# Second stage: the low parts of key tiles 3 and 7 are subtracted on GpSimd in place of VectorE

## The reference, cut to what matters

```python
def _L2_attn_ref(seq):
    attn = jnp.einsum('blc,bmc->blm', seq, seq)
    attn = jax.nn.softmax(attn, axis=2)
    return jnp.einsum('blm,bmc->blc', attn, seq)
...
t = t + _L2_attn_ref(_ln_t(t))
```

## Time and profile before

| | |
|---|---|
| median of 3 runs | 3016.01 us (3010.62 to 3026.71) |
| the profiled execution, its own time | 3013.47 us |
| its span, first to last instruction | 3011.3 us |
| VectorE busy over the span | 2327.7 us (77%) |
| PE busy | 2282.4 us (76%) |
| ScalarE busy | 2132.5 us (71%) |
| GpSimd busy | 1742.0 us (58%) |
| granted TensorE clock, mean over the span | 0.923 |
| `low`, line 1166, 256 instructions | 319.4 us, mean 1269 ns |
| the subtraction of the same shape on GpSimd in a later stage, line 1813, 256 instructions | 544.9 us, mean 2142 ns |

### The profile page before, as it was taken

One profiled execution on the slowest core, in us unless ns is written; L12 is line 12 of the kernel. 1 busy time (PEld: TensorE's weight loads), 2 busy tenths in 40 slices (PEclk: granted clock), 3 DMA queues, 4 the chain that ended last, 5 costly groups with the idle time before them and its releaser, 6 DMA issues. The chain is left out here.

```text
span 3011.3 us, 86006 instructions
## 1 busy us (share of the span) xinstructions
PE 2282.4 (76%) x33244; PEld 1642.6 (55%) x33244; DVE 2327.7 (77%) x3714; ACT 2132.5 (71%) x3776; POOL 1742.0 (58%) x1370
## 2 busy tenths in 40 slices
PE   3777777778774888888644585888888888777777
PEld 1555555555552655555433473776777676545444
DVE  3677778777774999999867325888888887688897
ACT  2677777777773999999722112888888887777776
POOL 3577777777764333333266202998999898733331
PEclk9999999999996999999957556999999999899999
DMA  3211111111100000000000200000000000000101
GB/s 72 49 44 42 36 37 39 42 42 31 27 16 4 18 17 14 17 17 15 12 1 1 52 5 2 9 5 5 6 7 5 5 7 7 4 22 21 24 21 25
DMA packets 144669, 62.22 MB, mean 21 GB/s; under 512 B 118676, under 2 KB 127798, under 8 KB 144566
## 3 DMA queue, kind: packets, MB, share of 16 engines
q1 hardware_dynamic: 139565, 58.00, 9.0%
q10 hardware_dynamic: 4393, 2.77, 0.4%
q0 software_dynamic: 608, 0.01, 0.0%
HBM read 14.50 MB, written 8.39 MB: 8 GB/s over the span
## 5 line engine op out<-in xcount | busy, mean ns | idle before, releaser
L1813 POOL TENSOR_TENSOR a_prl<-a_pr,a_prh 128x1024 f16<-128x1024 f32 x256 | 544.9, 2142 | 47.8 <-ACT a_prh L1790 46.1
L1730 DVE TENSOR_REDUCE a_nmax<-a_ps_a 128x1 f16<-128x1024 f32 x256 | 312.2, 1219 | 34.0 <-PE a_ps_a L1852 32.1
L1166 DVE TENSOR_TENSOR a_exl<-a_ex,a_exh 128x1024 f16<-128x1024 f32 x256 | 319.4, 1269 | 8.4 <-ACT a_exh L1219 6.2
L1213 ACT ACTIVATE a_ex<-a_ps_s,a_shift 128x1024 f32<-128x1024 f32 x256 | 281.5, 1101 | 21.1 <-DVE a_exl L1166 12.8
L1790 ACT ACTIVATE a_prh<-a_pr 128x1024 f16<-128x1024 f32 x256 | 270.6, 1057 | 8.1
L1868 PE MATMUL a_ps_s<-a_qx,a_kh 128*128 128x128 f16 x2048 | 259.1, 220 | 2.7 <-issue 2.6
L1786 ACT ACTIVATE a_pr<-a_ps_s 128x1024 f32<-128x1024 f32 x256 | 259.5, 1014 | 0.0
L1870 PE MATMUL a_ps_s<-a_qm,a_kl 128*128 128x128 f16 x2048 | 259.2, 220 | 0.0
L2115 ACT ACTIVATE f_mixed_s<-f_ps_e,f_gates 128x64 f32<-128x64 f32 x1024 | 212.7, 426 | 40.1 <-PE f_ps_e L395 37.2
L113 POOL TENSOR_TENSOR a_w_hl<-a_w_xn,a_w_hl 128x512 f16<-128x512 f32 (+1 forms) x64 | 82.4, 1288 | 273.2 <-ACT a_w_hl L106 273.2
L1274 PEld LDWEIGHTS a_ps_o<-a_w_hl,a_exh 128*128 128x128 f16 x2048 | 181.9, 98 | 91.2 <-DVE a_exl L1166 66.2
(11 more groups left out here) (344 smaller groups left out, 8526.7 us busy)
## 6 DMA issues: line engine op xcount, KB each, us to landing
tokens<-in_x_dram SPq DMA_DIRECT2D x32, 256.0 KB, 2.9
bl_qg<-bl_qk_high SPq DMA_DIRECT2D x128, 64.0 KB, 2.0
bl_km<-bl_qk_high SPq DMA_DIRECT2D x256, 32.0 KB, 2.0
a_xTb<-a_w_xT SPq DMA_DIRECT2D x64, 128.0 KB
out_dram<-tokens SPq DMA_DIRECT2D x32, 256.0 KB, 2.6
bl_qg<-bl_qk_low SPq DMA_DIRECT2D x64, 64.0 KB, 2.0
bl_km<-bl_qk_low SPq DMA_DIRECT2D x128, 32.0 KB, 2.0
a_qm<-a_qx SPq DMA_DIRECT2D x64, 64.0 KB, 2.0
```

Of the source, the lines that this page charges most:

```text
L1166: nc.vector.tensor_tensor(exl[:, at[2]], ex[:, r], exh[:, at[2]], ALU.subtract).then_inc(low, 1)
L1213: nc.scalar.activation(ex[:, r], ps_s[:, m % 2], ACT.Exp, bias=shift[:], accum_out=rs[at[1]][:, m:m + 1]).then_inc(exped, 1)
L1730: nc.vector.tensor_reduce(nmax[:, g:g + 1], ps_a[:], AX.X, ALU.max, negate=True).then_inc(maxed, 1)
L1813: nc.gpsimd.tensor_tensor(prl[:, r], pr[:, r], prh[:, r], ALU.subtract).then_inc(low, 1)
```

## The change

A tuple `POOL_LOW = (3, 7)` names two key tiles whose low part GpSimd now makes, with the same instruction and operands. GpSimd gets a `step` of its own with a lag of one tile: the low part of tile 7 of the image before stands at m=0, ahead of everything else of GpSimd in the image; that of tile 3 stands at m=4, behind lines 90 and 92 and ahead of `norm_apply`. It waits there for the high part. The semaphore `low` becomes two, `low_v` and `low_g`, and the function `low_count` gives for a tile which of the two to wait for and up to which count; ScalarE's ring and TensorE's products wait by it. Nothing else is changed; the last low part of the stage is made in the trailing steps (`lag` 1 for GpSimd's `stream`).

```diff
--- before.py
+++ after.py
@@ -1080,6 +1080,7 @@
 
     nc, sem = net.nc, net.sem
     RING, PARTS, LAG = 4, 8, 4
+    POOL_LOW = (3, 7)
     VECTOR_HIGH = (1, 4, 7)
     with ExitStack() as ctx:
         def sb(name, shape, dt):
@@ -1100,8 +1101,8 @@
         ln = net.norms[0]
         swapped, shift_set = (sem("a2_" + s) for s in ("swapped", "shift_set"))
 
-        scored, exped, high_s, high_v, low, weighed = (sem("a2_" + s) for s in (
-            "scored", "exped", "high_s", "high_v", "low", "weighed"))
+        scored, exped, high_s, high_v, low_v, low_g, weighed = (sem("a2_" + s) for s in (
+            "scored", "exped", "high_s", "high_v", "low_v", "low_g", "weighed"))
         inverted, normed, added = (sem("a2_" + s) for s in ("inverted", "normed", "added"))
         tv = net.t[:].rearrange("p (i h) g c -> p i h g c", h=2)
         base = net.normed
@@ -1119,6 +1120,15 @@
             if m in VECTOR_HIGH:
                 return high_v, len(VECTOR_HIGH) * (2 * i + h) + before
             return high_s, (NT - len(VECTOR_HIGH)) * (2 * i + h) + m + 1 - before
+
+        def low_count(at, lag=0):
+
+            i, h, m = at
+            m -= lag
+            before = len([k for k in POOL_LOW if k <= m % NT]) + m // NT * len(POOL_LOW)
+            if m % NT in POOL_LOW:
+                return low_g, len(POOL_LOW) * (2 * i + h) + before
+            return low_v, (NT - len(POOL_LOW)) * (2 * i + h) + m + 1 - before
 
         def past(at, lag):
 
@@ -1160,10 +1170,10 @@
 
                 def step(i, h, m):
                     at = tile_at(i, h, m - 1)
-                    if at:
+                    if at and at[2] not in POOL_LOW:
                         r = at[2] % RING
                         dve.wait_ge(*high_count(at))
-                        nc.vector.tensor_tensor(exl[:, at[2]], ex[:, r], exh[:, at[2]], ALU.subtract).then_inc(low, 1)
+                        nc.vector.tensor_tensor(exl[:, at[2]], ex[:, r], exh[:, at[2]], ALU.subtract).then_inc(low_v, 1)
                     at = now(i, h, m)
                     if at and at[2] in VECTOR_HIGH:
                         r = at[2] % RING
@@ -1207,7 +1217,7 @@
                         r = at[2] % RING
                         act.wait_ge(scored, count(at))
                         if past(at, RING):
-                            act.wait_ge(low, count(at, RING))
+                            act.wait_ge(*low_count(at, RING))
                         if at[2] == 0 and past(at, 2 * NT):
                             act.wait_ge(added, 2 * at[0] + at[1] - 1)
                         nc.scalar.activation(ex[:, r], ps_s[:, m % 2], ACT.Exp, bias=shift[:],
@@ -1234,7 +1244,14 @@
                     if k == 4:
                         norm_apply(nc, ln, n + 1, w, nc.gpsimd)
 
-                stream(pool, nothing, near, far, 0)
+                def step(i, h, m):
+                    at = tile_at(i, h, m - 1)
+                    if at and at[2] in POOL_LOW:
+                        r = at[2] % RING
+                        pool.wait_ge(*high_count(at))
+                        nc.gpsimd.tensor_tensor(exl[:, at[2]], ex[:, r], exh[:, at[2]], ALU.subtract).then_inc(low_g, 1)
+
+                stream(pool, step, near, far, 1)
 
             @block.tensor
             def _(pe):
@@ -1262,7 +1279,7 @@
                     at = tile_at(i, h, m - LAG)
                     if at:
                         ia, ha, k = at
-                        pe.wait_ge(low, count(at))
+                        pe.wait_ge(*low_count(at))
                         if k == 0 and past(at, 2 * NT):
                             pe.wait_ge(added, 2 * ia + ha - 1)
                         z_high, z_low = wk[ha]["hl"][:, k, 0:C], wk[ha]["hl"][:, k, C:2 * C]
```

## The result

The changed kernel takes 3052.65 us (median of 3 runs, 3050.76 to 3061.72) against 3016.01 us (3010.62 to 3026.71): ratio 1.013, 95% interval 1.0095 to 1.0164. It is slower by 36.6 us; 46 us were forecast.

The account below looks back on a forecast made before the run. VectorE was taken as the bound: +1.53 us over 28 images (42.8 us) plus the first and last images made +47.4 us on the profiled 3013.47, giving 3060.9, stated as 3062; range 3035 to 3085.

Parts of the forecast that it names:

- The bound: Second stage, steady part: VectorE bounds at 98% busy; without collisions ScalarE would be next at 15.3 to 15.7 us an image.
- The exclusion: GpSimd's subtraction shuts VectorE's `low`, casts, `centre` and `add` out of SBUF for 2.00 us, up to 4.0 us per image.
- Tile 7: Its low part on GpSimd, beside `sum` and `centre` at the image's start, adds 0.19 us an image; `centre` loses 1.46.
- Tile 3 with norm_apply: Subtraction before `add` delays it 1.57 us, net +0.44 an image; `norm_apply` then delays `low4`, +0.85.
- The cut: GpSimd's `cut_low` enters behind `low0` and costs `cast1` 0.96 us, +0.05 us an image over before.
- The ends: Outside the steady images: images 0 and 1 about +2 us together, image 30 +0.8, image 31 +0.9, last `low7` +0.9.
- The sum: All stage costs together +47.4 us on the profiled 3013.47 us, giving 3060.9; stated as 3062 for the median.
- The clock in the steady part: TensorE's share falls to 79% in the stage; granted clock stays 1.00, so nothing is charged.
- The other signs: Profile after: `norm_apply` right behind `low3`, GpSimd's new subtractions 2.1 us, 192 `low` costing little less than 256, clock 1.00.
- Partial cancelling: Rival: exclusion bites partly and cancels the gain, `norm_apply` and one `low` falling in gaps; within 15 us of 3013; chance 0.08.
- `norm_apply` staying hidden: Rival: `add` slips ahead of `low3` (margin 0.4 us) or ScalarE makes a gap; +0.68 us an image, about 3037; chance 0.17.
- nothing hidden: Rival: both new subtractions cost VectorE their full 2.00 us, +0.97 more an image, about 3088 us; chance 0.12.

Follow-up runs that it names:

- Left out, two low parts: Against the kernel before, the low parts of tiles 3 and 7 are made by no engine; waits go to the high parts: ratio 0.9929, 15.63 us an image.
- extra subtractions: Kernel before, all low parts on VectorE, plus two small additions and two scratch subtractions on GpSimd per image: 19.35 us an image, 3110.87 us, one run.
- extra fills: Kernel before plus two small additions and two scratch-buffer fills on GpSimd per image, nothing taken off VectorE: 17.19 us an image, 3050.43 us, one run.
- tile 3 alone: Against the kernel before, only the low part of tile 3 moves to GpSimd: ratio 1.0112, 17.34 us an image, 3040.96 us.
- low3 earlier: Changed kernel with GpSimd making the low part of tile 3 a step earlier, ahead of lines 90 and 92: 17.38 us an image, 3044.61 us, one run.

## Why the prediction held, and where it was off

- **The bound.** VectorE bound the stage and still does: 429.07 of 438.05 us before, 98% after. Left out, two low parts show ScalarE next at 15.63 us; the forecast had 15.3 to 15.7.
- **The exclusion.** Read from the earlier trace rows and shown by the pair of extra subtractions and extra fills. The hold of 2.00 us taken from the earlier trace rows holds: `centre` starts to work 1.99 us after GpSimd does. That `add` would be shut out too had no row in before; it is.
- **Tile 7.** +0.19 forecast (the 0.05 for the cut stood beside it), +0.14 measured alone.
- **Tile 3 with norm_apply.** 0.44 + 0.85 = 1.29 forecast, 1.12 measured alone. The low part starts 2.95 us after `low2` (1229.36 to 1232.31), not 3.06: I took the start of `norm_apply`, which needs the result of line 92 and starts 0.08 us after its end, while the low part needs nothing of it and starts 0.04 us before. That is 0.11 us; where the other 0.06 went I can't say, as the images of the kernel with tile 3 alone take 16.94 to 17.54 us.
- **The cut.** Forecast 0.96, measured 0.85 in most images (`low1` at 2.06), the same collision as before. Here the layout by hand placed `cut_low` 0.3 us too early, under `low0` instead of under `cast1`.
- **Per image** this makes 1.34 us where I had 1.53, and over 27 images 36.2 us where I had 41.3. This is the term that was too large.
- **The ends** were a little too small. By the yardstick of the sums the last stretch seems to grow by 6.3 us (46.22 to 52.53), but 1.27 us of that is only that `sum` comes earlier in the image once `low7` no longer stands ahead of it. From `cast7` to `cast7` the stage divides so: +2.9 us up to that of image 1 (2 forecast), +36.2 over 27 images (41.3), +5.1 to the end (4.1). In the end part image 30 takes 15.23 us in place of 14.26, image 31 14.40 in place of 13.24, and the way from the last `cast7` to the end 5.92 in place of 4.40.
- **The last 1.5 us.** 0.9 of them were forecast, as GpSimd's longer subtraction. The other 0.6 is the clock. TensorE had waited 1.93 us for that subtraction, and made the last 24 products of the stage at half the clock (0.50 granted, 1.2 GHz), in 1.46 us in place of 0.87. Before, then after, in the columns of the earlier trace rows:

```profile
1486.80:1487.90 1.10, 0.87 (x24) 0.76 (x24) 0.17 (x3) 0.00 (x0) 0.00 (x0) 1.00 0.00 0
1535.10:1536.80 1.70, 1.46 (x24) 1.30 (x24) 0.05 (x1) 0.00 (x0) 0.02 (x1) 0.50 0.00 0
```

- **The sum.** +47.4 us forecast for the stage, +44.1 measured in the profiles, +36.6 between the medians. The forecast's last step is loose: 3060.9 us and the 2.5 us by which the median lies above the profiled execution make 3063.4, not 3062. Of the 9.4 us between 3062 and 3052.65 the stage's terms explain 3.3; the rest lies outside the stage, where the forecast charged nothing and the profile of the changed kernel is 6.5 us shorter. That the forecast of the whole came this near is in part luck.
- **The clock in the steady part.** I charged nothing for it, because at 76% busy TensorE had been granted 1.00. The share did not carry over: in the changed kernel TensorE is busy 81% and the clock is 0.98 (0.96 to 1.00 in windows of 80 to 100 us); in the kernel with the extra subtractions it is 0.89 to 0.95. Nor is it the mean share alone: from 1100 to 1400 us the kernel with low3 earlier has TensorE as busy as the changed one (243.13 and 243.63 us) at 1.00 against 0.98; its longest wait for a low part is 1.7 us, that of the changed kernel 2.4. TensorE is not the bound there and VectorE is as busy as before, so I see no time lost to the clock in the steady part; no run isolates this.
- **The other signs.** `norm_apply` follows `low3` at once, the 64 subtractions of GpSimd take 2.15 us on average, and the 192 low parts of VectorE cost 281.4 us where the 256 cost 319.4. The clock is the one sign that did not come as written.
- **Partial cancelling, `norm_apply` staying hidden, nothing hidden:** none of the three came. `add` is issued 0.45 us after the low part of tile 3 begins, the margin forecast as 0.4.

## What to carry to other kernels

When an elementwise instruction with two SBUF inputs moves from VectorE to GpSimd, cost the move by the time for which GpSimd holds the streams against what VectorE has next in its order that GpSimd does not hold up, which here were the reductions and what reads PSUM, but not the casts, and follow what the new instruction pushes back in GpSimd's own queue. Busy shares (GpSimd at 34%) say nothing of this. The same move can be made to pay by putting this work of VectorE in one row and gating GpSimd to start with it; the gain then ends where the next engine is the bound.

## What the runs showed of the hardware

- A GpSimd fill of 128x2304 (2.01 us) leaves VectorE's two-input instructions at full speed (0.69 and 1.22 us); a GpSimd subtraction of about the same length stretches `centre` from 0.69 to 2.07 us. No row of the kernel before showed this.
- The root of line 92, 128x8, takes 1.64 us and shuts VectorE out for none of it that shows: in the changed kernel `cast4` ran under it at 0.67 us (1231.10). What holds VectorE is not the span of a GpSimd instruction as such.
- After a wait of 1.93 us TensorE was granted half its clock, and 24 products took 1.46 us in place of 0.87.
- A GpSimd instruction starts 0.08 us after one whose result it needs, and 0.04 us before the reported end of one that it does not need (1230.71 + 1.64 against 1232.31).
